# The last ten ticks of an attention pipeline in another order

## What is computed

```python
x = x + jnp.tanh(g_xattn[0]) * _L0_xattn_ref(_layernorm(x, axis=-1), ctx_4096, mask, ...)   # 32 heads, 8 KV heads, head size 128
x = x + jnp.tanh(g_ffn[0]) * _L0_ffn_ref(_layernorm(x, axis=-1), up, down, perm)            # 16 small per-head FFNs, features permuted
x = x + jnp.tanh(g_xattn[1]) * _L1_xattn_ref(_layernorm(x, axis=-1), ctx_4096, ctx_4096, ...)
x = x + jnp.tanh(g_ffn[1]) * _L1_ffn_ref(_layernorm(x, axis=-1), gate_w, ...)               # 8 experts, one per token
```

## Time and profile before

| | us |
|---|---|
| median of 3 runs (773.26 to 774.77) | 773.93 |
| the profiled execution | 777.05 |
| its span (first to last instruction) | 775.3 |
| PE busy | 749.7 (97%) |
| DVE busy | 458.3 (59%) |
| ACT busy | 428.8 (55%) |
| POOL busy | 277.0 (36%) |
| share of PE in the chain that ended last | 88% |
| mean granted clock of TensorE, share of full | 0.983 |

### The profile page before, as it was taken

One profiled execution on the slowest core, in us unless ns is written; L12 is line 12 of the kernel. 1 busy time (PEld: TensorE's weight loads), 2 busy tenths in 40 slices (PEclk: granted clock), 3 DMA queues, 4 the chain that ended last, 5 costly groups with the idle time before them and its releaser, 6 DMA issues.

```text
span 775.3 us, 12432 instructions
## 1 busy us (share of the span) xinstructions
PE 749.7 (97%) x3875; PEld 593.0 (76%) x3875; DVE 458.3 (59%) x1017; ACT 428.8 (55%) x1274; POOL 277.0 (36%) x436
## 2 busy tenths in 40 slices
PE   8999999999999999999999999999999999887997
PEld 7888887888787887878888878787787645476875
DVE  4796403546556555555555655646558876777643
ACT  3753326566556556556656555655555565656831
POOL 0531006244235235233424423523312457614333
PEclk9999999999999999999999999999999999996999
DMA  8546451402321041140140123203142145825142
GB/s 311 179 146 183 138 181 56 192 14 68 110 97 69 14 178 47 50 177 27 55 190 14 68 80 126 69 14 124 35 156 79 55 143 177 327 115 192 44 116 75
DMA packets 40654, 87.04 MB, mean 112 GB/s; under 512 B 5497, under 2 KB 25465, under 8 KB 36626
## 3 DMA queue, kind: packets, MB, share of 16 engines
q1 hardware_dynamic: 37540, 78.45, 28.9%
q0 software_dynamic: 3056, 7.89, 2.9%
HBM read 70.02 MB, written 35.05 MB: 136 GB/s over the span
## 4 chain that ended last, share of the span: by engine, by line
PE 88%; DVE 4%; ACT 3%; POOL 2%; issue 1%; DMA 1%; POOLq 0%; SPq 0%; DVEq 0%; ACTq 0%
PE banks L970 8%; PE banks L972 7%; PE banks L1004 7%; PE banks L971 7%; PE banks L1006 7%; PE banks L1005 7%; PE banks L954 7%; PE banks L991 3%; PE banks L436 3%; PE banks L434 3%; PE banks L435 3%; PE banks L983 2%; PE banks L1961 2%; PE banks L1960 2%; PE banks L1962 2%; PE banks L1015 2%
## 5 line engine op out<-in xcount | busy, mean ns | idle before, releaser
L638 ACT ACTIVATE p_sb<-p_sb,nmax 128x128 f32<-128x128 f32 x256 | 99.7, 391 | 56.7 <-DVE nmax L858 56.7
L633 ACT ACTIVATE oT_hi<-banks 128x512 fp32r<-128x512 f32 x64 | 38.2, 596 | 132.7 <-PE banks L1017 132.6
L895 DVE SCALAR_TENSOR_TENSOR x_sb<-banks,tgates,x_sb 128x512 f32<-128x512 f32 x64 | 48.0, 750 | 63.1 <-PE banks L1006 63.1
L750 POOL TENSOR_TENSOR v_lo<-v_raw,v_hi 128x128 fp32r<-128x128 f32 x64 | 29.5, 461 | 125.3 <-ACT v_hi L681 125.3
L853 DVE SCALAR_TENSOR_TENSOR p_sb<-banks,q_rstd,mask 128x128 f32<-128x128 f32 x256 | 71.4, 341 | 2.5 <-POOL q_rstd L89 2.4
L755 POOL TENSOR_TENSOR p_sb<-p_sb,rsum 128x512 f32<-128x512 f32 x64 | 66.6, 1041 | 15.1 <-DVE rsum L885 15.1
L954 PEld LDWEIGHTS banks<-kT,qT_sb 128*128 128x128 f32 x512 | 66.9, 191 | 5.3
L954 PE MATMUL banks<-kT,qT_sb 128*128 128x128 f32 x512 | 67.3, 275 | 0.0
L842 DVE TENSOR_TENSOR oT_lo<-banks,oT_hi 128x512 fp32r<-128x512 f32 x64 | 44.1, 689 | 31.8 <-ACT oT_hi L633 31.8
L885 DVE RECIPROCAL rsum<-prob_sum 128x4 f32<-128x4 f32 x64 | 11.3, 177 | 80.7 <-ACT p_sb L638 80.7
L889 DVE TENSOR_TENSOR pT_lo<-banks,pT_hi 128x512 fp32r<-128x512 f32 x64 | 44.2, 690 | 23.1 <-ACT pT_hi L656 23.1
(11 more groups left out here) (297 smaller groups left out, 1906.3 us busy)
## 6 DMA issues: line engine op xcount, KB each, us to landing
sorted_x<-in_empty SPq DMA_DIRECT2D x8, 2064.0 KB, 10.3
w_raw<-in_wq_l SPq DMA_DIRECT2D x8, 1024.0 KB, 5.4
w_raw<-in_wo_l SPq DMA_DIRECT2D x8, 1024.0 KB, 4.8
exp_w<-in_exp_w_l SPq DMA_DIRECT2D x8, 1024.0 KB, 8.8
kT_scr<-kT_st SPq DMA_DIRECT2D x16, 256.0 KB, 2.4
v_scr<-v_st SPq DMA_DIRECT2D x16, 256.0 KB, 2.5
xs<-sorted_x SPq DMA_DIRECT2D x15, 258.0 KB, 2.8
v_raw<-v_scr SPq DMA_DIRECT2D x14, 256.0 KB, 2.5
```

What stands on the lines that cost most here:

```text
L638: last = act.activation(p_sb[:, b % 2, h * P:(h + 1) * P], p_sb[:, b % 2, h * P:(h + 1) * P], ACT.Exp, bias=nmax[:, b % 2, h:h + 1], accum ...
L895: dve.scalar_tensor_tensor(out=s.x[:, b, :], in0=o_ps[b % 2][:, :], scalar=s.tgates[:, 0:1], in1=s.x[:, b, :], op0=ALU.mult, op1=ALU.add). ...
```

## The change

The lists of PE, DVE and ACT for the last ten ticks are written anew; all else stays. No instruction is added or removed.

- **PE**: `scores` of unit t+1 instead of t, placed behind `values` (`only(DRAIN, scores)` does unit 58 in tick 58, so that none is missed). `o_proj` of unit t-2 is done in two halves of six products (two heads each): `o_first` ahead of `values`, `o_second` behind `scores`. `transpose_x` stands behind `values`, and `transpose_x45` behind the whole output products instead of ahead of them.
- **ACT**: `oT_split` of unit t-1 at the end of tick t's attention work instead of unit t-2 at its start (the same place in the stream), but ahead of the z and x copies; `v_split` behind `exps` and `q_seed`.
- **DVE**: `pT_split` first, then `x_stats` of unit t-3 instead of t-2, `p_recip`, the picks, `oT_split` of t-1, `mask_max` of t+1, `accumulate`.

```diff
--- before.py
+++ after.py
@@ -560,6 +560,16 @@
             for b in range(4):
                 step(G, 0, b)
 
+        DRAIN = UNITS - QAHEAD
+
+        def only(unit, stage):
+
+            def entry(u, b, g, odd):
+                if u == unit:
+                    stage(u, b, g, odd)
+
+            return entry
+
         LN2_LAST = {HB - 1: slice(0, HB), HB + 1: slice(HB, HB + 2), B - 1: slice(HB + 2, B)}
         C45 = LN2_LAST[HB + 1]
 
@@ -739,8 +749,8 @@
             weights = [(wq_split(kt), 10 - kt) for kt in range(KT)] + [(wo_split(h), 4 - h) for h in range(HG)]
             run(act, [(oT_split, -2), (qT_copy, 5), (square, 5)] + weights
                 + [(exps, 0), (q_seed, 4), (pT_split, -1), (v_split, 2), (split_bias, 0)],
-                [(oT_split, -2), (qT_copy, 5), (square, 5), (pT_split, -1), (v_split, 2), (exps, 0), (q_seed, 4), (copy_z01, 0),
-                 (copy_xT, -4), (copy_z23, -2), (seed_ln2, -3), (seed_ln2_45, -3), (copy_xT4, -4)],
+                [(only(DRAIN - 2, oT_split), -2), (qT_copy, 5), (square, 5), (pT_split, -1), (exps, 0), (q_seed, 4), (v_split, 2),
+                 (oT_split, -1), (copy_z01, 0), (copy_xT, -4), (copy_z23, -2), (seed_ln2, -3), (seed_ln2_45, -3), (copy_xT4, -4)],
                 [(qT_copy, 5), (square, 5)] + weights + [(pT_split, -1), (exps, 0), (v_split, 2)])
 
         @block.gpsimd
@@ -938,8 +948,9 @@
 
             run(dve, [(oT_split, -2), (mask_max, 0), (pick_sums, 4), (q_half, 4), (p_recip, 0), (pT_split, -1),
                       (accumulate, -2), (x_stats, -2), (split_bias, 0)],
-                [(oT_split, -2), (mask_max, 0), (normalise_ln2, -4), (pT_split, -1), (pick_sums, 4), (q_half, 4),
-                 (p_recip, 0), (normalise_ln2_45, -3), (copy_xT5, -4), (accumulate, -2), (copy_xT, -4), (x_stats, -2)],
+                [(only(DRAIN - 2, oT_split), -2), (only(DRAIN, mask_max), 0), (pT_split, -1), (normalise_ln2, -4), (x_stats, -3),
+                 (p_recip, 0), (pick_sums, 4), (q_half, 4), (oT_split, -1), (mask_max, 1), (normalise_ln2_45, -3),
+                 (copy_xT, -4), (accumulate, -2), (copy_xT5, -5)],
                 [(mask_max, 0), (pT_split, -1), (p_recip, 0)])
 
         @block.tensor
@@ -993,18 +1004,29 @@
                 last.then_inc(pT_done, 1)
 
             def o_proj(u, b, g, odd):
-                pe.wait_ge(oT_lo_done, u + 1)
-                reached(pe, acc_done, u - 1)
-                if after(u, b, g, B - 3):
-                    pe.wait_ge(s.z_copied[1], 2)
-                for h in range(HG):
+                o_heads(u, b, g, odd, 0, HG)
+
+            def o_first(u, b, g, odd):
+                o_heads(u, b, g, odd, 0, HG // 2)
+
+            def o_second(u, b, g, odd):
+                o_heads(u, b, g, odd, HG // 2, HG)
+
+            def o_heads(u, b, g, odd, lo, hi):
+                if lo == 0:
+                    pe.wait_ge(oT_lo_done, u + 1)
+                    reached(pe, acc_done, u - 1)
+                    if after(u, b, g, B - 3):
+                        pe.wait_ge(s.z_copied[1], 2)
+                for h in range(lo, hi):
                     if b == 0:
                         pe.wait_ge(wo_lo_done, 4 * g + h + 1)
                     oh, ol = oT_hi[:, h * P:(h + 1) * P], oT_lo[:, h * P:(h + 1) * P]
                     pe.matmul(o_ps[b % 2][:, :], oh, wo_hi[odd][:, h, :], start=(h == 0), stop=False)
                     pe.matmul(o_ps[b % 2][:, :], ol, wo_hi[odd][:, h, :], start=False, stop=False)
                     last = pe.matmul(o_ps[b % 2][:, :], oh, wo_lo[odd][:, h, :], start=False, stop=(h == HG - 1))
-                last.then_inc(o_done, 1)
+                if hi == HG:
+                    last.then_inc(o_done, 1)
 
             def values(u, b, g, odd):
                 pe.wait_ge(pT_lo_done, u + 1)
@@ -1071,8 +1093,9 @@
             pe.matmul(oT_ps[:, 0:P], s.wt[:, :], s.wzT[:, :], start=True, stop=True).then_inc(mT_done, 1)
             pe.wait_ge(s.v_copied, 2 * B - 1)
             run(pe, [(scores, 0), (sum_squares, 4), (q_proj, 6), (p_transpose, -1), (o_proj, -2), (values, -1)],
-                [(scores, 0), (sum_squares, 4), (z01, 0), (p_transpose, -1), (z2, -1), (transpose_x45, -4), (o_proj, -2),
-                 (transpose_x, -4), (values, -1), (z3, -1)])
+                [(only(DRAIN, scores), 0), (sum_squares, 4), (z01, 0), (p_transpose, -1), (z2, -1),
+                 (o_first, -2), (values, -1), (transpose_x, -4), (z3, -1), (scores, 1), (o_second, -2),
+                 (transpose_x45, -4)])
 
 
 def middle(nc, d, s, block):
```

## The result

| | before | after |
|---|---|---|
| median, us (runs) | 774.35 (4) | 792.73 (4) |
| lowest to highest | 773.26 to 776.39 | 792.12 to 795.04 |
| profiled execution, us | 777.05 | 792.63 |
| its span, us | 775.3 | 790.8 |
| first `up` (trace time) | 629.76 | 648.21 |

What follows compares the result with a forecast made beforehand. PE was taken to bound the kernel, with 88% of the chain of waits. Ring and fringes 15.7 (63.4 - 47.2 - 0.5) plus clock 2.2 gave 17.9 on the median 773.9: 791.8 us, range 789.0 to 796.5.

Steps and rivals of the forecast that it cites:

- The ring: Plain ticks: ACT's copy into the one oT_hi waits for the second six, holding up DVE, then PE; 7.6 us against 6.0.
- rival E: Last ten ticks: the covering works as drawn and PE's 5.2 us of waits go at best, 768.7 us; chance 0.03.
- 58 to 59: Distance between these units' values: the mask of unit 60 needs new factors through DVE, ACT and POOL; 8.9 us.
- 60 to 61: Distance between these units' values: z01 waits for accumulate of unit 59, PE idle 3.98 us; 10.7 us.
- 62 to 63: Distance between these units' values, through POOL's layer norm, transposes, second six, ACT's copies and z; 9.3 us.
- 63 to `up`: From values of unit 63 to the first `up`, through oT copies, output products, transposes and z; 11.7 us.
- The start: Values of unit 57 come earlier than before, by 0 to 1.4 us; taken as 0.5.
- Clock: Last ten ticks: two stretches of low clock at the two long PE idle times; 2.2 us, ends 0 and 7.7.
- Rival B: Last ten ticks: the clock stays up, idle times being short or cut by work; 789.6 us, chance 0.20.
- rival C: Last ten ticks: the clock falls in every tick, costing 7.7 us; 797.3 us, chance 0.08.
- The tail: POOL's gathers for batches 4 and 5 come 4 us later against PE; cost taken as 0, ends 0 and 2.0.
- rival D: Behind `up`: the gathers become late and add 2.0 us; 793.8 us, chance 0.10.

Runs made afterwards that it cites:

- e2_two: The changed kernel, order untouched, with a second pair of buffers for oT_hi and oT_lo from unit 57 on; 780.32 us, 1.0077 of before.
- e6_split: The kernel before with only the output products split in two sixes, the second behind the values; 783.97 us, 1.0111 of before.
- e9_acc: The changed kernel with DVE's accumulate of t-2 moved ahead of oT_lo of t-1 and the mask; 787.67 us, 1.0165 of before.
- e1_whole: The changed kernel with the twelve output products in one piece ahead of the values; 782.87 us, 1.0094 of before.
- e4_fill: The changed kernel with eight more z products, results unread, put into PE's wait for accumulate of unit 59; 796.68 us, 1.0268 of before.
- e3_zlate: The changed kernel with the first pair of z products moved to the end of its tick, behind the second six; 792.19 us, 1.0205 of before.

## Why the prediction was right, point by point

- **The ring** (7.6 us per plain tick against 6.0): 7.73, 7.73, 7.72. That ACT waits for the second six and not the values, DVE 3.1 ahead of `oT_lo`, PE ahead of the values: all in the rows above. PE's waits in the plain tick are 1.03 and 1.34, put at 1.1 and 1.6. With ACT's wait rival E (the covering works) fell. e2_two, e6_split and e9_acc show that it is a ring through one buffer, that the split makes it, and that DVE's steps in it count in full. The term was 0.1 short per tick: behind an idle PE the second product of the values starts 0.34 after the first (597.96, 598.30 in the trace) and not 0.23.
- **58 to 59**, new factors: 8.9 put, 8.81 measured. The mask of unit 60 waits for POOL's last step, as the sum had it, and starts 8.79 behind that of unit 59:

```profile
594.80 1.13 DVE L863 SCALAR_TENSOR_TENSOR p_sb<-banks,q_rstd,mask 128x128 f32<-128x128 f32 x4 [0.97 <-POOL q_rstd L89]
```

- **60 to 61**, z01 behind accumulate: the wait was put at 3.98 and is 3.98. The tick was put at 10.7 and is 13.28; 2.3 of the difference is the low clock, 0.3 the ring's parts.
- **62 to 63**: 9.3 put, 9.64. **63 to `up`**: 11.7 put, 11.88.
- **The start**: values of 57 0.5 earlier against the scores before them, 0.53 measured.
- **Clock**: 2.2 put, as two stretches of 1.1. It was one, and cost 2.3. That this term came out is luck, two errors that cancel: the stretch was twice as long as that of the earlier trace rows (0.66 over 10 us is 6.8 us at the half clock), and behind the wait z products, transposes and the first output products stood in it in a row, not the 4.8 of 7.6 of a plain tick. The waits in the tick of 8.8 left the clock up in this execution. Rival B (clock full throughout) and rival C (the clock falls in every tick, 7.7) both fell. The Trainium skill, page "TensorE: Matmul & The Clock Gate", section "HAM oscillation — how this bites in real kernels", describes clocks that fall again and again between bursts; here it was once or twice in seven ticks in the change, in e1_whole to e4_fill and in e9_acc, and in e6_split, with PE idle for 0.7 and 1.0 us in each plain tick, never.
- **The tail** (0): the gathers for batches 4 and 5 start 3.2 us behind `up`, 1.4 ahead of it before: 4.6 later, where 4 was said. PE then waits 0.73 for what is read back, a wait that the trace of before does not have. So rival D's mechanism is there, at a third of its 2.0, and the medians don't show it. POOL's row and PE's:

```profile
651.41 0.94 POOL L1298 DMA_INDIRECT xg<-xT_scr,perm_col  x1 [4.75 <-DMA xT_scr<-xT]
```

```profile
675.86 1.09 PE L1452 MATMUL banks<-ident_sb,xT 128*128 128x128 f32 x8 [0.73 <-DMA xT<-yT_scr]
```

- **Behind `up`** the profiled executions differ by more: 142.6 us to the end of the span against 145.5 in before. The change need not have a part in that: over all eleven traces this part lasts 142.6 to 145.5 us, without order in the changes made ahead of it. The granted clock was 0.86 over the 75 us from 640 in the profiled execution of before, which stands 3.1 above the median of 773.93, and 0.93 over the 75 us from 658 in this one. Medians differ by 18.4, as `up` does (18.45).

```profile
640.00:715.00 75.00, 64.43 (x381) 42.77 (x374) 56.28 (x167) 45.81 (x81) 36.15 (x56) 0.86 0.53 199
```

```profile
658.00:733.00 75.00, 63.06 (x390) 40.31 (x390) 57.67 (x168) 47.36 (x84) 38.80 (x58) 0.93 0.57 212
```

- **Sum**: 17.9 put. By the trace the distances give 66.8 - 47.2 - 0.5 = 19.0. The changed trace was 0.6 us earlier already at the scores ahead of the change (577.50, before 578.09), which makes the 18.45 at `up`; by the median it is 18.4 (17 to 20). Without the clock the distances are 64.5 where 63.4 was put, so the ring and its fringes were 1.1 short.

What remains open is what makes the clock fall where. In e3_zlate and e4_fill PE's rows from 560 to 598 lie within 0.04 us of the change's, and in both the clock fell right behind the wait of 2.21 there; in the change's own execution it did not. Their first 20 us differ by up to 1.3 us, so the executions are not the same from the start. No last idle time decides it: 1.35 and 1.50 stood beside the beginning of low stretches in e9_acc and e2_two, 1.49 and 1.76 in e6_split ahead of none.

## What to carry to other kernels

Before a stage is split around another to cover a wait, list for each of its operands how many buffers there are and who waits for its last reader: with one buffer, what was put between first and last reader was added here to every turn of the ring, together with what stood in the queues of the engines that refill it. Add up that ring from single durations; here the sum came within 0.1 us of the tick, and moving one step of 0.7 out of it gave 0.65 back in each. And cover small waits by taking what is late out of the way (accumulate and statistics on DVE, the layer norm on POOL, together 1.3 to 3.2 us here), before the work on the full engine is cut up.

## What the runs showed of the hardware that I had not expected

- The same instructions at the same times just before do not settle whether the granted clock falls: of three executions with PE's rows within 0.04 us of each other from 560 to 598 us, two fell behind the wait of 2.21 and one stayed up until 611, inside the wait of 3.98.
- A stretch at the lower level can be 6.8 us long here, and cost 2.3 us where PE had work in a row for the rest of it (z to values 6.04 against 3.74), twice the 1.1 that I had put. The stretch at 598 in e3_zlate and e4_fill cost 1.6 (9.32 against 7.73).
- A 128x512 product of f32 as z's is two records in the trace and together 0.86 us long, as the rows of before had it too (3.52 for four); the first output product behind an idle PE takes 0.50 where one in a row takes 0.39.
